# Loading and multiplying the first tiles of x and W by halves of columns

## The chip, the cores and the metric

The kernel runs on one core of a Trainium2 chip. The metric is the device time of one execution in microseconds (us), and the kernel's time is the median of several executions.

## The reference

Four layers with residuals, in float32, on x of shape (32, 64, 1024). What is computed, cut to what matters:

```python
x = x + einsum('bct,bcd->bdt', x, L0_w[itok_B_0_15])          # 16 matrices of 64x64
x = x + einsum('bct,bcd->bdt', x, L1_w[itok_B_0_15])          # 16 matrices of 64x64
x = x + einsum('bsi,oi->bso', x, W) + low_rank(x, A[itok_B_0_2], B) * 0.5   # W is 1024x1024
x = x + einsum('bsi,boi->bso', x, L3_w[itok_B_3_7])           # 8 matrices of 1024x1024
```

The indices pick a matrix for each of the 32 batches. A residual becomes an identity matrix added to the weights.

## The kernel before, in words

A float32 product is made of three matmuls in the faster fp32r type: each operand is split into a high part (a copy rounded to fp32r) and a low part (the operand less its high part), and hi·hi, hi·lo and lo·hi are summed in PSUM. High parts are made mostly by ScalarE (ACT; `w_hi`, `x_hi`), low parts by VectorE (DVE; `w_lo`, `x_lo`).

The third layer's product with W comes first in the program. It works on transposed tiles: W in blocks of four tiles of 128x512 (`w_slot`), x in blocks of four tiles of 128x512 (`x_slot`), and one block product is 4 outputs (`o`) x 4 tiles (`k`) x 3 parts = 48 matmuls of 128x512. The blocks are combined as in a fast 2x2 matrix product, with the sums S1 to S4 and T1 to T4. Low-rank terms (`low_rank`, L1400) and deltas (L1412) go between. The fourth layer follows from some 182 us on (L1517), with each batch's own matrix, and the first two layers, joined to one 64x64 matrix per index (L1449 makes these), are applied to its result (`mix`, L1543).

Every engine runs its own program, and what orders them are semaphores, written by hand. A wait stands in an engine's program and holds everything behind it there. At the start:

- **SP (the sync engine)** issues the loads in the order of its code, L307 to L322: for each of the four tiles k of the first W block and the first x block a load of 256 KB, the loads of the two small layers' weights (`w1_s`, `w0_s`, 256 KB each) behind k = 1, then `load_x(1, 1, 1)` (1 MB, the second x block), `lora_a`, `load_x(2, 2, 0)`, `lora_b`, `load_w(1, 1, 2)` and two more blocks of W. There is no wait among them.
- **ACT** issues five loads of its own, L564 to L568: the first tile of x, the identity `eye`, the indices `toks`, and `asked` and `cells`, which the plan of the fourth layer is made from. Then comes its first activation, L662, ahead of which the compiler has put a table load, and which makes the high part of columns 128 to 511 of W's tile k = 0 (`w_hi_off`). Columns 0 to 127 follow (L664, `w_hi`) when DVE has added the identity to them. For k = 1 to 3 it makes `w_hi` and `x_hi` (L573, L576).
- **DVE** casts the first tile of x (L878, `x_hi`), waits for the identity, and goes through k = 0 to 3: `x_lo`, the identity added to the next tile of W (`diagonal`, L1179, semaphore `A11`), `w_lo`, and for k = 1 and 2 `plus_eye` (L886, semaphore `w01i`), which adds identities to `w1_s` and `w0_s`. At k = 2 and 3 it also loads four indices each into registers (L1194). `x_los(1)` follows, the second x block's low part (L906), and later the selection of low-rank matrices (L1204).
- **PE (TensorE)** multiplies zeros (`warm`, L1354, WARM = 15 matmuls of 128x256 on the tile `st`), then makes the first product (L1439): for each k the four hi·hi, the four hi·lo, the four lo·hi. For k = 0 it takes the outputs in the order 1, 2, 3, 0, since output 0 needs the columns with the identity. L1449 joins the two small layers (it waits for `w01i`), and the next product (L1373 to L1375) waits for the low parts of the second x block.

`cells` and `asked` are waited for by the semaphore `consts`, just ahead of the first steps of the plan (DVE, L1219), and `eye` by DVE ahead of `diagonal(0)`.

## Time and profile before

| | us |
|---|---|
| median of 3 runs | 383.66 (383.42 to 383.82) |
| the profiled execution's own time | 382.85 |
| its span, first to last instruction | 381.05 (the page rounds to 381.1) |
| PE busy in the span | 375.2 |
| first matmul of zeros | 1.35 |
| first matmul of the first product | 5.03 |
| start of L1449, behind the first product | 16.64 |

The span is 1.8 us shorter than the execution's own time, and that execution was 0.81 us below the median of the runs. Times inside the trace are counted from the start of the span. A busy PE is not PE at its peak: matmuls are pipelined, so the distance from one start to the next tells more than the duration of one.

### The profile page before, as it was taken

To read this page: it belongs to the slowest core of one execution; us is meant where nothing else is said; L and a number is where in the kernel's file an instruction comes from. 1 tells how busy PE (TensorE), PEld (TensorE's weight loads), DVE (VectorE), ACT (ScalarE), POOL (GpSimd) and SP (SyncE) were. 2 spreads that over 40 slices of the span, in tenths; PEclk is the share of its full clock that TensorE was granted. 3 is DMA by queue.
4 is the path that set the end of the run, shared out by engine and by line. 5 is a ranking of instruction groups with operands and counts; after the bars stand their busy time and mean duration, and the time that the engine had idled before them with its cause. 6 is when DMAs were issued, how large, how long until landed. Compare 5 with 4: busy or idle time off the path is not lost.

```text
span 381.1 us, 7667 instructions
## 1 busy us (share of the span) xinstructions
PE 375.2 (98%) x1733; PEld 312.9 (82%) x1734; DVE 268.4 (70%) x301; ACT 224.7 (59%) x299; POOL 116.4 (31%) x157
## 2 busy tenths in 40 slices
PE   8999999999999999999999999999999999999995
PEld 7888888888888888888888888888888888888884
DVE  4786978846849788537868467963599635999653
ACT  4689577487246475245475465753677536779433
POOL 0000231000000000024765347763167532676500
PEclk9999999999999999999999999999999999999999
DMA  8976905640278384406428316552256522664223
GB/s 286 397 281 212 341 0 193 208 151 9 104 251 279 133 330 139 169 26 215 161 71 252 86 28 206 192 164 58 57 190 210 160 58 58 207 201 151 60 65 85
DMA packets 24187, 61.38 MB, mean 161 GB/s; under 512 B 1906, under 2 KB 2098, under 8 KB 24114
## 3 DMA queue, kind: packets, MB, share of 16 engines
q1 hardware_dynamic: 23648, 60.10, 47.7%
q8 instruction: 29, 0.48, 0.5%
q10 hardware_dynamic: 466, 0.44, 0.4%
q14 instruction: 44, 0.36, 0.3%
HBM read 52.15 MB, written 8.39 MB: 159 GB/s over the span
## 4 chain that ended last, share of the span: by engine, by line
PE 98%; ACT 1%; ACTq 1%; issue 0%
PE ps L1517 45%; PE ps L1373 12%; PE ps L1374 12%; PE ps L1375 12%; PE ps L1400 4%; PE ps L1543 4%; PE ps L1439 3%; PE ps L1609 2%; PE ps L1412 2%; PE ps L1558 1%; ACT L662 0%; PE ps L1449 0%; ACTq L566 0%; ACT ring L662 0%; ACTq L568 0%
## 5 line engine op out<-in xcount | busy, mean ns | idle before, releaser
L1517 PE MATMUL ps<-ring,aT 128*128 x752 | 173.1, 389 | 0.0
L1517 PEld LDWEIGHTS ps<-ring,aT 128*128 128x128 f32 x752 | 141.1, 188 | 29.5 <-issue 0.2
L1373 PE MATMUL ps<-ring 128*128 128x512 f32 x208 | 81.1, 390 | 0.0
L1374 PE MATMUL ps<-ring 128*128 128x512 f32 x208 | 81.0, 389 | 0.0
L1375 PE MATMUL ps<-ring 128*128 128x512 f32 x208 | 80.9, 389 | 0.0
L476 POOL TENSOR_TENSOR aT<-xT,aT 128x512 fp32r<-128x512 f32 (+1 forms) x36 | 55.5, 1562 | 46.8 <-ACT aT L761 41.6
L1266 DVE TENSOR_TENSOR ring<-raw,ring 128x1024 f32 (+1 forms) x40 | 63.2, 1639 | 5.9 <-ACT ring L747 5.9
L767 ACT ACTIVATE aT<-ps 64x1024 fp32r<-64x1024 f32 x32 | 32.7, 1023 | 48.5 <-PE ps L1517 48.2
L1294 DVE TENSOR_TENSOR stage<-ps,stage 64x1024 f32<-64x1024 f32 x30 | 36.7, 1222 | 27.7 <-ACT stage L776 27.0
L1283 DVE TENSOR_TENSOR aT<-ps,aT 64x1024 fp32r<-64x1024 f32 x32 | 39.1, 1223 | 21.4 <-ACT aT L767 20.7
L1373 PEld LDWEIGHTS ps<-ring 128*128 128x128 f32 x208 | 39.1, 188 | 8.1
L1375 PEld LDWEIGHTS ps<-ring 128*128 128x128 f32 x208 | 39.0, 188 | 8.1
L1374 PEld LDWEIGHTS ps<-ring 128*128 128x128 f32 x208 | 39.1, 188 | 7.9
L776 ACT ACTIVATE stage<-ps 64x1024 f32<-64x1024 f32 x30 | 30.5, 1018 | 23.8 <-PE ps L1543 23.4
L747 ACT ACTIVATE ring<-raw 128x1024 f32 (+1 forms) x40 | 39.2, 1046 | 6.0 <-POOL raw L468 3.5
L630 ACT ACTIVATE xT<-ps 128x512 f32<-128x512 f32 x40 | 22.4, 593 | 20.0 <-PE ps L1375 19.7
L525 POOL MEMSET st<- 128x512 f32 x1 | 0.5, 525 | 100.3 <-ACT low_split L623 100.3
L468 POOL TENSOR_TENSOR raw<-raw,eye 128x128 f32<-128x128 f32 x40 | 18.9, 485 | 25.3 <-DMA raw<-w3t 22.4
L906 DVE TENSOR_TENSOR ring<-ring_f,ring 128x1024 fp32r<-128x1024 f32 (+1 forms) x20 | 21.5, 1113 | 5.1 <-ACT ring L576 5.1
L761 ACT ACTIVATE aT<-xT 128x512 fp32r (+1 forms) x36 | 20.0, 601 | 3.2 <-DVE xT L987 2.8
L576 ACT ACTIVATE ring<-ring_f 128x1024 fp32r<-128x1024 f32 (+1 forms) x19 | 17.9, 984 | 6.2 <-DMA ring_f<-xt 3.6
L490 POOL CAST st<-aT 128x64 fp32r x32 | 18.7, 583 | 8.8 <-POOL st L492 6.5
(95 smaller groups left out, 329.2 us busy)
## 6 DMA issues: line engine op xcount, KB each, us to landing
raw<-w3t SPq DMA_DIRECT2D x40, 512.0 KB, 4.3
ring_f<-xt SPq DMA_DIRECT2D x8, 1024.0 KB, 7.9
raw<-xt SPq DMA_DIRECT2D x8, 1024.0 KB, 5.2
out<-stage SPq DMA_DIRECT2D x30, 256.0 KB, 3.2
ring_f<-wt SPq DMA_DIRECT2D x4, 1024.0 KB, 8.0
xT<-xt SPq DMA_DIRECT2D x3, 1024.0 KB, 10.2
xT<-wt SPq DMA_DIRECT2D x2, 1024.0 KB, 16.0
ring_f<-wt SPq DMA_DIRECT2D x4, 256.0 KB, 4.7
```

What stands on the lines that cost most here:

```text
L476: pool.tensor_tensor(x3_split(i, ks, P + h * T, T), xT[:, ks, bass.ds(which[h] * T, T)], as_f32(x3_split(i, ks, h * T, T)), ALU.subtract). ...
L630: act.activation(dst[:, o, :], ps_l2(phase, j, o), ACT.Copy).then_inc(s(name), 1)
L747: act.activation(dst, adapter_raw(t), ACT.Copy).then_inc(s("w_hi"), 1)
L767: act.activation(r_tile(h)[own, :], acc(p)[own, :, :].rearrange("p a n -> p (a n)"), ACT.Copy)\
L776: act.activation(stage[own, p, :], mixed_ps[h][other, :, :].rearrange("p a n -> p (a n)"), ACT.Copy)\
L1266: dve.tensor_tensor(in_two(unit_of(t, 1)), adapter_raw(t), as_f32(in_two(unit_of(t, 0))), ALU.subtract)\
L1283: dve.tensor_tensor(r_tile(h)[other, :], acc(p)[own, :, :].rearrange("p a n -> p (a n)"), as_f32(r_tile(h)[own, :]), ALU.subtract).then_in ...
L1294: dve.tensor_tensor(dst, mixed_ps[h][own, :, :].rearrange("p a n -> p (a n)"), dst, ALU.add)\
L1373: pe.matmul(dst, hi_of(qw)[:, k, cs], hi_of(qx)[:, k, :], start=start and k == 0, stop=False, skip_group_check=True)
L1374: pe.matmul(dst, hi_of(qw)[:, k, cs], lo_of(qx)[:, k, :], start=False, stop=False, skip_group_check=True)
L1375: last = pe.matmul(dst, lo_of(qw)[:, k, cs], hi_of(qx)[:, k, :], start=False, stop=stop and k == HALF - 1, skip_group_check=True)
L1517: last = pe.matmul(acc(i)[:, n, :], x3_split(i, k, start, P), ring[:, bass.ds(off + (part * D + n * 512), 512)], start=(k == 0 and j == 0) ...
```

## The change

It touches only the beginning of each engine's program.

1. The first tile (k = 0) of W and that of x are loaded in two halves of 256 columns each (`FRONT`), W's second half first. The semaphores are `w_front1`, `w_front0`, `x_front0`, `x_front1`. Both queues so issue one more load ahead of what followed.
2. On SP, tiles k = 1 to 3 follow at once, and `w1_s`, `w0_s` come behind them. `asked` and `cells` move from ACT's queue to SP's, behind `w0_s` and ahead of `load_x(1, 1, 1)`.
3. ACT makes the high part of W's columns 256 to 511 as soon as they are there, and then of 128 to 255. Each raises `w_hi_off` by one.
4. DVE casts x by halves, makes `x_lo` of tile 0 before it waits for the identity, and does both `plus_eye` behind the last tile's `w_lo`.
5. PE has 12 matmuls of zeros in place of 15, and in the first product for k = 0 outputs 2 and 3 (W's second half) come first, each in two matmuls of 256 columns for hi·hi. Output 1 follows, then hi·lo of 2, 3 and 1, both for output 0, and lo·hi in the order 2, 3, 1, 0. From k = 1 on the order is as before.

```diff
-WARM = 15
+WARM = 12
+FRONT = slice(0, 256), slice(256, 512)
...
-            for k in range(HALF):
+            for half in (1, 0):
+                sp.dma_start(raw_of(w_slot(0))[:, 0, FRONT[half]], wt[1, 1, 0][:, FRONT[half]]).then_inc(s(f"w_front{half}"), 16)
+            for k in range(1, HALF):
                 one = slice(k, k + 1)
                 sp.dma_start(raw_of(w_slot(0))[:, one, :], w_block(1, 1)[:, one, :]).then_inc(s(f"w_in0_{k}"), 16)
-
-                if k:
-                    sp.dma_start(raw_of(x_slot(0))[:, one, :], x_block(1, 0)[:, one, :]).then_inc(s(f"x_in0_{k}"), 16)
-                if k == 1:
-                    sp.dma_start(w1_s, w1).then_inc(s("w1"), 16)
-                    sp.dma_start(w0_s, w0t).then_inc(s("w0"), 16)
+                sp.dma_start(raw_of(x_slot(0))[:, one, :], x_block(1, 0)[:, one, :]).then_inc(s(f"x_in0_{k}"), 16)
+            sp.dma_start(w1_s, w1).then_inc(s("w1"), 16)
+            sp.dma_start(w0_s, w0t).then_inc(s("w0"), 16)
+            sp.dma_start(asked[:, :], indices[:, 2, :].to_broadcast([B, B])).then_inc(s("consts"), 16)
+            sp.dma_start(cells[:, 0:C_SIZE], plan_c).then_inc(s("consts"), 16)
...
-            act.dma_start(raw_of(x_slot(0))[:, 0, :], xt[0, 1, 0]).then_inc(s("x_in0_0"), 16)
+            for half in range(2):
+                act.dma_start(raw_of(x_slot(0))[:, 0, FRONT[half]], xt[0, 1, 0][:, FRONT[half]]).then_inc(s(f"x_front{half}"), 16)
             act.dma_start(eye[:, :], eye_c).then_inc(s("eye"), 16)
             act.dma_start(toks[:, :, :], indices).then_inc(s("toks"), 16)
-            act.dma_start(asked[:, :], indices[:, 2, :].to_broadcast([B, B])).then_inc(s("consts"), 16)
-            act.dma_start(cells[:, 0:C_SIZE], plan_c).then_inc(s("consts"), 16)
...
-            act.wait_ge(s("w_in0_0"), 16)
-            act.activation(hi_of(w_slot(0))[:, 0, P:], raw_of(w_slot(0))[:, 0, P:], ACT.Copy).then_inc(s("w_hi_off"), 1)
+            for half, cols in ((1, FRONT[1]), (0, slice(P, 2 * P))):
+                act.wait_ge(s(f"w_front{half}"), 16)
+                act.activation(hi_of(w_slot(0))[:, 0, cols], raw_of(w_slot(0))[:, 0, cols], ACT.Copy).then_inc(s("w_hi_off"), 1)
...
-            dve.wait_ge(s("x_in0_0"), 16)
-            dve.tensor_copy(hi_of(x_slot(0))[:, 0, :], raw_of(x_slot(0))[:, 0, :]).then_inc(s("x_hi"), 1)
-            dve.wait_ge(s("eye"), 16)
+            for half, raised in enumerate(("x_hi_front", "x_hi")):
+                dve.wait_ge(s(f"x_front{half}"), 16)
+                dve.tensor_copy(hi_of(x_slot(0))[:, 0, FRONT[half]], raw_of(x_slot(0))[:, 0, FRONT[half]]).then_inc(s(raised), 1)
...
+            x_lo(0, None, slice(0, 1))
+            dve.wait_ge(s("eye"), 16)
             diagonal(0)
...
-                if k in (1, 2):
-                    plus_eye(k - 1)
+                if k == HALF - 1:
+                    plus_eye(0)
+                    plus_eye(1)
...
+            pe.wait_ge(s("w_hi_off"), 1)
+            pe.wait_ge(s("x_hi_front"), 1)
+            for o in (2, 3):
+                part(o, 0, 0, 0, FRONT[0], True)
+            pe.wait_ge(s("x_hi"), 1)
+            for o in (2, 3):
+                part(o, 0, 0, 0, FRONT[1])
+            pe.wait_ge(s("w_hi_off"), 2)
+            part(1, 0, 0, 0, start=True)
+            pe.wait_ge(s("x_lo"), 1)
+            for o in (2, 3, 1):
+                part(o, 0, 0, 1)
+            pe.wait_ge(s("w_hi"), 1)
+            part(0, 0, 0, 0, start=True)
+            part(0, 0, 0, 1)
+            pe.wait_ge(s("w_lo"), 1)
+            for o in (2, 3, 1, 0):
+                part(o, 0, 1, 0)
```

ACT's program from its first load to its first three activations, before (ring_f is the memory that W and x are loaded to, ring that of the split parts):

```order
L564 DMA ring_f<-xt 128x512
L565 DMA eye<-eye_c 128x192
L566 DMA toks<-indices 1x96
L567 DMA asked<-indices 32x32
L568 DMA cells<-plan_c 32x81
L662 ACT_TABLE_LOAD
L662 ACTIVATE ring<-ring_f 128x384 [waits w_in0_0]
L664 ACTIVATE ring<-ring_f 128x128 [waits A11]
L573 ACTIVATE ring<-ring_f 128x512 [waits A11]
```

The same stretch of ACT's program in the changed kernel:

```order
L567 DMA ring_f<-xt 128x256 x2
L568 DMA eye<-eye_c 128x192
L569 DMA toks<-indices 1x96
L664 ACT_TABLE_LOAD
L664 ACTIVATE ring<-ring_f 128x256 [waits w_front1]
L664 ACTIVATE ring<-ring_f 128x128 [waits w_front0]
L666 ACTIVATE ring<-ring_f 128x128 [waits A11]
L574 ACTIVATE ring<-ring_f 128x512 [waits A11]
```

Two loads stand no longer ahead of the table load, one more half of x does, and the first activation has become two.

PE's program from the matmuls of zeros to the second tile (k = 1) of the first product, before:

```order
L1354 MATMUL ps<-st 128x256 [waits zeroed]
L1354 MATMUL ps<-st 128x256 x14
L1439 MATMUL ps<-ring 128x512 [waits x_hi,w_hi_off]
L1439 MATMUL ps<-ring 128x512 x2
L1439 MATMUL ps<-ring 128x512 [waits w_hi]
L1439 MATMUL ps<-ring 128x512 [waits x_lo]
L1439 MATMUL ps<-ring 128x512 x3
L1439 MATMUL ps<-ring 128x512 [waits w_lo]
L1439 MATMUL ps<-ring 128x512 x3
L1439 MATMUL ps<-ring 128x512 [waits x_hi,w_hi]
```

The same stretch of PE's program in the changed kernel:

```order
L1360 MATMUL ps<-st 128x256 [waits zeroed]
L1360 MATMUL ps<-st 128x256 x11
L1430 MATMUL ps<-ring 128x256 [waits x_hi_front,w_hi_off]
L1430 MATMUL ps<-ring 128x256
L1430 MATMUL ps<-ring 128x256 [waits x_hi]
L1430 MATMUL ps<-ring 128x256
L1430 MATMUL ps<-ring 128x512 [waits w_hi_off]
L1430 MATMUL ps<-ring 128x512 [waits x_lo]
L1430 MATMUL ps<-ring 128x512 x2
L1430 MATMUL ps<-ring 128x512 [waits w_hi]
L1430 MATMUL ps<-ring 128x512
L1430 MATMUL ps<-ring 128x512 [waits w_lo]
```

Columns multiplied are as many as before. The wait for `w_hi`, which needs the identity, stood behind three matmuls of 512 columns and stands now behind what makes six of them.

DVE's program at tile k = 0, in the changed kernel (before, L1179, the identity's addition with its wait for `eye`, stood ahead of the first L906, which is L908 here):

```order
L881 CAST ring<-ring_f 128x256 [waits x_front0]
L881 CAST ring<-ring_f 128x256 [waits x_front1]
L908 TENSOR_TENSOR ring<-ring_f,ring 128x512 [waits x_hi]
L1181 TENSOR_TENSOR ring_f<-ring_f,eye 128x128 [waits w_front0,eye]
L1181 TENSOR_TENSOR ring_f<-ring_f,eye 128x128 [waits w_in0_1]
L901 TENSOR_TENSOR ring<-ring_f,ring 128x512 [waits w_hi]
```

## Rows read from the trace of the kernel before

**Rows 1.** The page: span, busy time of PE, and 40 slices of the span
```profile
span 381.1 us, 7667 instructions
...
PE 375.2 (98%) x1733; PEld 312.9 (82%) x1734; DVE 268.4 (70%) x301; ACT 224.7 (59%) x299; POOL 116.4 (31%) x157
...
PE   8999999999999999999999999999999999999995
```

**Rows 2.** The chain that ended last: start us, us, what
```profile
3.11 1.28 ACT L662
4.39 0.01 issue
4.40 0.53 ACT ring L662
4.94 0.09 issue
5.03 11.68 PE ps L1439 x48
16.71 1.09 PE ps L1449 x16
...
182.16 16.32 PE ps L1517 x72
```

**Rows 3.** Timeline of ACT's queue: start us, us, engine, line, what
```profile
0.79 0.41 ACTq L564 DMA_DIRECT2D ring_f<-xt  x1
1.24 0.44 ACTq L565 DMA_DIRECT2D eye<-eye_c  x1
...
2.28 0.32 ACTq L567 DMA_DIRECT2D asked<-indices  x1
...
2.64 0.44 ACTq L568 DMA_DIRECT2D cells<-plan_c  x1
...
5.80 0.31 ACT L664 ACTIVATE ring<-ring_f 128x128 fp32r<-128x128 f32 x1 [0.88 <-DVE ring_f L1179]
```

**Rows 4.** Timeline of DVE at the first product
```profile
4.45 0.43 DVE L878 CAST ring<-ring_f 128x512 fp32r<-128x512 f32 x1 [4.34 <-DMA ring_f<-xt]
...
5.48 0.29 DVE L1179 TENSOR_TENSOR ring_f<-ring_f,eye 128x128 f32<-128x128 f32 x1 [0.60 <-DMA eye<-eye_c]
5.69 0.69 DVE L906 TENSOR_TENSOR ring<-ring_f,ring 128x512 fp32r<-128x512 f32 x1
...
15.36 2.36 DVE L906 TENSOR_TENSOR ring<-ring_f,ring 128x1024 fp32r<-128x1024 f32 x2 [1.30 <-ACT ring L576]
```

**Rows 5.** Timeline of PE in small windows: zeros, then the first product's start
```profile
1.35 3.57 PE L1354 MATMUL ps<-st 128*128 128x256 f32 x15 [1.35 <-POOL st L457]
...
1.94 1.05 PE L1354 MATMUL ps<-st 128*128 128x256 f32 x4
...
5.59 0.84 PE L1439 MATMUL ps<-ring 128*128 128x512 f32 x2
...
6.02 0.65 PE L1439 MATMUL ps<-ring 128*128 128x512 f32 x2
```

**Rows 6.** DMA issues in small windows: KB each, us from issue to landing
```profile
ring_f<-wt SPq DMA_DIRECT2D x1, 256.0 KB, 3.5
ring_f<-xt ACTq DMA_DIRECT2D x1, 256.0 KB, 3.6
...
eye<-eye_c ACTq DMA_DIRECT2D x1, 96.0 KB, 4.2
...
ring_f<-wt SPq DMA_DIRECT2D x1, 256.0 KB, 4.1
```

**Rows 7.** Stretches: us, busy us of PE, PEld, DVE, ACT, POOL; PEclk, DMA share, GB/s
```profile
1.80:2.20 0.40, 0.40 (x4) 0.40 (x4) 0.00 (x0) 0.00 (x0) 0.00 (x0) 1.00 0.97 108
2.20:2.60 0.40, 0.40 (x4) 0.40 (x4) 0.00 (x0) 0.00 (x0) 0.00 (x0) 1.00 0.85 215
2.60:3.00 0.40, 0.40 (x3) 0.40 (x3) 0.00 (x0) 0.00 (x0) 0.00 (x0) 1.00 0.75 266
3.00:3.40 0.40, 0.40 (x3) 0.40 (x3) 0.00 (x0) 0.29 (x1) 0.00 (x0) 1.00 0.99 374
3.40:3.80 0.40, 0.40 (x4) 0.40 (x3) 0.00 (x0) 0.40 (x1) 0.00 (x0) 1.00 1.02 384
...
6.00:10.00 4.00, 4.00 (x19) 3.14 (x18) 3.37 (x8) 2.42 (x5) 0.00 (x0) 1.00 1.03 391
```

More of the change, by code:

```diff
@@ L1176, in diagonal @@
             def diagonal(k):
-                dve.wait_ge(s(f"w_in0_{k}"), 16)
+                dve.wait_ge(s(f"w_in0_{k}" if k else "w_front0"), 16)
                 d = raw_of(w_slot(0))[:, k, P * k:P * (k + 1)]
                 dve.tensor_tensor(d, d, eye[:, 0:P], ALU.add).then_inc(s("A11"), 1)
+            x_lo(0, None, slice(0, 1))
+            dve.wait_ge(s("eye"), 16)
             diagonal(0)
@@ L1184, in _ @@
                 one = slice(k, k + 1)
-                x_lo(0, None, one)
+                if k:
+                    x_lo(0, None, one)
                 if k < HALF - 1:
@@ L1422, in _, with part @@
             w, x = (hi_of(w_slot(0)), lo_of(w_slot(0))), (hi_of(x_slot(0)), lo_of(x_slot(0)))
-            for k in range(HALF):
-                for a, b in ((0, 0), (0, 1), (1, 0)):
-                    high = (a, b) == (0, 0)
-                    if high and k == 0:
-                        pe.wait_ge(s("w_hi_off"), 1)
-                        pe.wait_ge(s("x_hi"), 1)
-                    elif high:
-                        pe.wait_ge(s("w_hi"), k + 1)
-                        pe.wait_ge(s("x_hi"), k + 1)
-                    elif b:
-                        pe.wait_ge(s("x_lo"), k + 1)
-                    else:
-                        pe.wait_ge(s("w_lo"), k + 1)
-                    for o in (1, 2, 3, 0) if high and k == 0 else range(HALF):
-                        if high and k == 0 and o == 0:
-                            pe.wait_ge(s("w_hi"), 1)
-                        last = pe.matmul(ps_l2(0, 0, o), w[a][:, k, P * o:P * (o + 1)], x[b][:, k, :],
-                                         start=high and k == 0, stop=k == HALF - 1 and a == 1, skip_group_check=True)
-                        if k == HALF - 1 and a:
-                            last.then_inc(s("l2"), 1)
+            def part(o, k, a, b, cols=slice(0, CT), start=False):
+                return pe.matmul(ps_l2(0, 0, o)[:, cols], w[a][:, k, P * o:P * (o + 1)], x[b][:, k, cols],
+                                 start=start, stop=k == HALF - 1 and a == 1, skip_group_check=True)
@@ new lines, in _ @@
+            part(0, 0, 0, 0, start=True)
[3 more added lines that the diff above has]
+                part(o, 0, 1, 0)
+            for k in range(1, HALF):
+                pe.wait_ge(s("w_hi"), k + 1)
+                pe.wait_ge(s("x_hi"), k + 1)
+                for o in range(HALF):
+                    part(o, k, 0, 0)
+                pe.wait_ge(s("x_lo"), k + 1)
+                for o in range(HALF):
+                    part(o, k, 0, 1)
+                pe.wait_ge(s("w_lo"), k + 1)
+                for o in range(HALF):
+                    last = part(o, k, 1, 0)
+                    if k == HALF - 1:
+                        last.then_inc(s("l2"), 1)
```

## The prediction

> **What bounds the kernel now.** I read the page first. PE is busy for 375.2 of 381.1 us, and in every slice but the first and the last it stands at 9 tenths [rows 1]. So an edit at the start is worth what it takes off the time at which PE gets through its first work, as long as no later wait takes it back. The chain of waits says what holds PE until 5.03 us [rows 2]: ACT's table load from 3.11 us, the copy that makes the high part of W's first tile from 4.40, 0.09 us to the matmul, and then 48 matmuls in 11.68 us. Ahead of the table load stand ACT's five DMA issues, from 0.79 on [rows 3]. DVE's branch is as long: its cast starts at 4.45, when x has landed, and ends at 4.88 [rows 4]. Both must get shorter for a gain.
>
> Next, PE's pace. In the fourth layer 72 matmuls of 512 columns take 16.32 us [rows 2], 0.227 us each. That is the 2.4 GHz level. The matmuls of zeros have 256 columns and start (1.05 - 0.415) / 3 = 0.21 us apart [rows 5], which is the 1.2 GHz level (0.415 us is what a single one lasts: 1.05 is three steps and one duration), although the column PEclk shows 1.00 [rows 7]. The first product starts at 5.03, the next matmuls at 5.59 and 6.02, the fourth at 6.27 [rows 2, 5]. The steps are 0.56, 0.43 and 0.25: two matmuls at the lower level, the first with 0.13 us on top, and the higher level from about 6.02 to 6.05 us, some 4.7 us after PE's first matmul. **So PE is slow where the change makes it start earlier**, and time won there is worth about half. From 6.27 on, 45 matmuls at 0.227 would end at 16.48; L1449 follows at 16.64. Later waits in this product cost 0.1 us at most.
>
> **The change, part by part.**
>
> *ACT's queue.* Two DMA issues leave, 0.32 and 0.44 us with 0.03 between (0.82). One more half of x comes, as long as the first (0.41 + 0.04), since an issue's time hardly follows its size: 96 KB take 0.44, 10 KB also 0.44 [rows 3]. The table load so starts 0.37 us earlier, at 2.74, and ends at 4.02. Bounds for the new issue: 0.32 and 0.44, that is 4.0 or 4.05.
>
> *The first copy of W.* 384 columns take 0.52 us [rows 2] and 128 take 0.31 [rows 3], so 256 take 0.42. It ends at 4.44 if W's half is there by 4.02. The matmul came 0.11 us behind the old copy's start plus 0.52, so the first one is now at **4.55 in place of 5.03**.
>
> *Do the halves land in time?* The whole tiles land at 0.77 + 3.5 = 4.3 (W) and 0.79 + 3.6 = 4.4 (x) [rows 6]. From 1.8 us on DMA moves 108, 215, 266, 374 and 384 GB/s in steps of 0.4 us [rows 7]. The sum reaches 256 KB, two halves, at some 3.05 us, and 512 KB, both tiles, at 3.75; landing is 0.5 to 0.7 us behind that. If bytes decide, the first halves land near 3.7 and the second ones at 4.3 and 4.4. If the number of loads decides, halves land where the first and second loads of each queue do now: 4.3 and 4.4, then 1.22 + 4.1 = 5.3 (the second on SP's queue) and 1.24 + 4.2 = 5.4 (`eye`, the second on ACT's) [rows 3, 6]. I take the bytes, as the rates climb to what the queues move later, 391 GB/s [rows 7].
>
> The Trainium skill speaks against splitting here ("DMA: Bandwidth & Descriptors", section Bandwidth): it wants loads of 1 MiB or more, with 64 KB at 138 GB/s against 341 for 1 MB, measured for loads that GpSimd issues. At 138 GB/s the four halves would take 3.8 us, and by that estimate the kernel would lose about 1 us. This trace doesn't agree for loads that queue up: with pieces of 256 KB in the queues it moves 391 GB/s [rows 7]. 128 KB it doesn't show.
>
> *DVE's casts.* 512 columns take 0.43 us [rows 4]. A half takes between 0.21 and 0.43. I take 0.28. The first ends at about 4.0 and does not bind, the second at 4.4 + 0.3 = 4.7.
>
> *PE in the first product.* At the lower level: first half matmul at 4.55, the next at 4.90 (0.21 + 0.13), then 5.11 (its `x_hi` is there at 4.8), 5.32, output 1 at 5.54, hi·lo at 5.96. The clock has risen meanwhile, so the next one starts at about 6.21. By then the equivalent of 4 matmuls of 512 columns is done. Before it was 3 at 6.27. **Gain: 0.06 + 0.227 = 0.28 us.** The half matmuls add no columns. Three matmuls of zeros fewer only make room: 12 of them let PE go at 1.35 + 0.38 + 11 x 0.21 = 4.1, ahead of 4.55; 15 would have held it until 4.72.
>
> *Waits behind it.* `x_lo` takes 0.69 [rows 4]: 4.75 to 5.44, asked for at 5.96. `eye` lands at 5.4 to 5.5 as now, since as many bytes are ahead of it, or at 6.0 if it counts as third load. Then diagonal 0.29 and ACT's copy 0.31 give `w_hi` at 6.2 (6.6), asked for at 6.67. `w_lo` (0.69) is there at 7.0 (7.3), asked for at 7.12, so between nothing and 0.2 us is lost. DVE has `x_lo` now ahead of the identity, so PE is not held by that. Tiles 2 and 3 land two loads earlier, which wins nothing, since PE did not wait for them.
>
> *What lands later.* SP issues one half, `asked` and `cells` more before the second x block, some 1.2 us of issue time; that block is issued at about 6.4 in place of 5.2 and still stands in a queue that is full until 10 us (391 GB/s) [rows 7], so it lands as before or 0.1 later. Both `plus_eye` now stand ahead of `x_los(1)`, 1.4 us of DVE. Before, DVE idled for 1.30 us ahead of that step [rows 4] while its sequencer loaded indices, so this is covered. If it were not, `x_los(1)`, which now starts at 15.36 and has its first half at 16.6, would have it at 18.0 in the worst case; PE asks at 17.4, so 0.6 us would be lost. `cells` is wanted only beyond 31 us.
>
> Sum: 381.05 - 0.28 = 380.77 us of span, 382.57 of own time. The profiled execution was 0.81 below the median, so the forecast for the median is 383.66 - 0.28 = **383.38 us**.
>
> **Rivals.**
>
> *B, more than half comes through.* If PE stands at the higher level when the product starts, the two slow matmuls vanish as well: 0.48 + 0.56 (1.24 us for three starts against 0.68) = 1.04 us, 382.6. It needs a rise before 4.6 us. Against it: in this trace PE had worked since 1.35 and was still slow at 5.6 [rows 5]. For it: one execution is all I see, and the runs differ by 0.4 us among themselves and by up to 1 from this one.
>
> *C, the second halves land late* (the number of loads decides; here stands the skill's rule). The first matmul is then at 4.8 (x's half at 4.4, cast 0.28, 0.1). x's second half lands at 5.4 and is cast at 5.7, hi·hi of outputs 2 and 3 ends at 6.2, output 1 at 6.4, `x_lo` is there at 6.5, three matmuls to 7.2, two to 7.65, `w_lo` at 7.75 because `eye` came at 6.0, four to 8.65. Before, twelve matmuls had been passed at 6.27 + 9 x 0.23 = 8.35. That is 0.3 us slower: 383.95. It decides if halves land more than 0.6 us behind the wholes.
>
> *D, slower: the clock rises later.* There are three matmuls of zeros fewer and a new pause, 4.1 to 4.55 us, against 0.3 us before. Each us at the lower level costs 1 - 0.227/0.427 = 0.47 us. If the pause made PE start its wait anew, the rise would come 4.7 us behind 4.55, at 9.2 in place of 6.0: + 1.5 - 0.28 = 1.2 us, 384.9. It outweighs the gain from 0.6 us of delay on, and is a loss over 0.2% from 2.2 us. Against it: a pause of 0.3 us (4.72 to 5.03) did no harm, and the work begins at the same 1.35. The Trainium skill ("TensorE: Matmul & The Clock Gate", part 1) says that the monitor runs freely and does not start anew with the kernel. By that rule the moment of the rise wanders from run to run in both kernels and D is unlikely; one trace cannot show it.
>
> *E, nothing is won*, because the table load doesn't end earlier or the stretch at 17 us gives it back: 383.66, inside the forecast's own range.
>
> **How the numbers follow.** A difference of 0.2% (0.77 us) is about what a measurement can tell from none. The forecast with E has 0.62, and its gains run from 0 to 0.6 us; 0.03 of it I give to gains above 0.77. B has 0.17, C 0.12, D 0.09. So faster 0.20, same 0.59 + 0.12 = 0.71, slower 0.09. The range reaches down to B (382.6) and up past C with the 0.2 us by which the runs differ from their median (384.2).
>
> **What would show it.** In the changed profile: the table load starts near 2.74 and the first product at 4.55, the steps of the first matmuls are 0.35, 0.21, 0.21, 0.21, 0.43, then 0.23, with the change of level near 6.0, and L1449 starts at 16.35. Wrong would be: halves of x that land after 4.8 (C), steps of 0.43 beyond 6.5 us (D), a first step of 0.12 (B), idle PE ahead of L1449 or of the second product (the moved `plus_eye`), or a gain at 16.6 that is gone by 182 us.

## The result, and the profile of the changed kernel

| | before | changed |
|---|---|---|
| median, us | 383.56 (382.80 to 383.82, 14 runs) | 383.87 (383.29 to 385.07, 14 runs) |
| profiled execution's own time / span, us | 382.85 / 381.05 | 383.86 / 382.0 |
| first matmul of the first product | 5.03 | 4.54 |
| start of the two small layers' join (L1449, now L1471) | 16.64 | 17.28 |
| start of the last matmul | 376.46 | 377.40 |

The ratio of the changed kernel to the one before is 1.0017, 95% interval 1.0010 to 1.0024. So the changed kernel is **slower**: by 0.3 us if the two medians are compared, by 0.65 us if the ratio is taken, which is not the quotient of the two medians (that is 1.0008). Either is less than the 0.2% which the prediction calls no difference, and the time is inside its range, but the sign is not the one forecast, and the interval of the ratio excludes 1. The two profiled executions are 1.0 us apart, because that of before was a quick one (0.7 us below its median); the changed kernel's stands at its median.

The page of the changed kernel, for [rows 1]:

```profile
span 382.0 us, 7669 instructions
...
PE 375.2 (98%) x1732; PEld 311.8 (82%) x1733; DVE 267.3 (70%) x302; ACT 225.2 (59%) x300; POOL 116.6 (31%) x157
...
PE   7999999999999999999999999999999999999995
```

PE has the same work in a longer span, and the one slice that differs is the first, 7 tenths in place of 8. The chain of waits, for [rows 2], names what fills it:

```profile
1.71 4.83 DMA eye<-eye_c
6.57 0.30 DVE ring_f L1181
6.90 0.32 ACT ring L666
7.26 10.09 PE ps L1430 x42
17.35 1.09 PE ps L1471 x16
...
182.81 16.32 PE ps L1539 x72
```

The table load and the first copy of W are gone from the chain. In their place stands one transfer, the identity's, issued at 1.71 us and landed at 6.55, then the addition, the copy and PE at 7.26. The 72 matmuls at the head of the fourth layer start 0.65 us later than before and take the same 16.32: nothing of the start is taken back, and nothing is added between. From the join to the last matmul the two executions need 360.12 and 359.82 us, and those of the experiments 359.8 to 360.2, with one exception told below, so 0.3 us there is scatter.

The timeline of the changed kernel (start us, us, engine, line, what, and in brackets the idle time before and its releaser), for [rows 3 to 5]:

```profile
1.71 0.45 ACTq L568 DMA_DIRECT2D eye<-eye_c  x1
...
2.78 1.28 ACT L664 ACT_TABLE_LOAD   x1 [2.65 <-issue]
...
3.50 0.29 DVE L881 CAST ring<-ring_f 128x256 fp32r<-128x256 f32 x1 [3.39 <-DMA ring_f<-xt]
...
4.07 0.61 ACT L664 ACTIVATE ring<-ring_f 128x256 fp32r<-128x256 f32 x2
4.43 0.30 DVE L881 CAST ring<-ring_f 128x256 fp32r<-128x256 f32 x1 [0.64 <-DMA ring_f<-xt]
...
4.54 1.93 PE L1430 MATMUL ps<-ring 128*128 128x256 f32 x8 [0.26 <-ACT ring L664]
...
4.76 0.69 DVE L908 TENSOR_TENSOR ring<-ring_f,ring 128x512 fp32r<-128x512 f32 x1
...
6.57 0.49 DVE L1181 TENSOR_TENSOR ring_f<-ring_f,eye 128x128 f32<-128x128 f32 x2 [1.12 <-DMA eye<-eye_c]
...
7.26 10.09 PE L1430 MATMUL ps<-ring 128*128 128x512 f32 x42 [0.79 <-ACT ring L666]
...
14.39 1.29 DVE L888 TENSOR_TENSOR stage<-stage,eye 128x512 f32<-128x512 f32 x2
...
15.85 2.36 DVE L908 TENSOR_TENSOR ring<-ring_f,ring 128x1024 fp32r<-128x1024 f32 x2 [0.17 <-issue]
```

The start did what the change says: table load at 2.78, casts of 0.29 and 0.30 us, first product at 4.54. Then DVE sits idle for 1.12 us and PE for 0.79 until the identity has come. Both `plus_eye` (1.29 us) lie ahead of `x_los(1)`, which starts at 15.85 with 0.17 us of idle time before it: covered.

PE in small windows (a row lists the matmuls that touch its window; its first number is the start of the first of them):

```profile
4.54 0.63 PE L1430 MATMUL ps<-ring 128*128 128x256 f32 x3 [0.26 <-ACT ring L664]
...
4.76 0.75 PE L1430 MATMUL ps<-ring 128*128 128x256 f32 x4
...
5.12 0.88 PE L1430 MATMUL ps<-ring 128*128 128x512 f32 x2
...
5.84 0.63 PE L1430 MATMUL ps<-ring 128*128 128x512 f32 x2
...
7.60 0.88 PE L1430 MATMUL ps<-ring 128*128 128x512 f32 x2
...
7.98 0.73 PE L1430 MATMUL ps<-ring 128*128 128x512 f32 x2
...
8.32 0.86 PE L1430 MATMUL ps<-ring 128*128 128x512 f32 x3
```

The second row starts at 4.76 and the third, three starts on, at 5.12: 0.12 us for a matmul of 256 columns, where the zeros of [rows 5] took 0.21. The trace records the rise of the granted clock at 4.57, so in this execution PE stood at the 2.4 GHz level from its first product matmul on. The last of the eight matmuls that can go without the identity starts at 6.08; 0.23 us behind it, at 6.31, PE wants `w_hi` and gets it at 7.26. That is **0.95 us of waiting**.

From there the whole loss can be added up. The eight matmuls are as many columns as six of 512, and before PE was through six at 6.27 + 3 x 0.23 = 7.0. So at 6.31 PE is 0.69 us ahead: 0.49 of it come from the earlier start, the rest from the clock. Then it waits 0.95. The next three steps, from 7.26 to 8.32, take 1.06 us where three at 0.23 take 0.69, so 0.37 more are lost. In the middle of them PE waits for `w_lo`, which DVE starts only at 7.24, when `w_hi` is there, and which takes 0.69:

```profile
7.24 0.69 DVE L901 TENSOR_TENSOR ring<-ring_f,ring 128x512 fp32r<-128x512 f32 x1 [0.17 <-ACT ring L666]
```

The sum is -0.69 + 0.95 + 0.37 = +0.63 us, and the join is 0.64 late.

The issues of the changed kernel (KB each, us from issue to landing), for [rows 6]:

```profile
ring_f<-xt ACTq DMA_DIRECT2D x2, 128.0 KB, 2.9
...
ring_f<-wt SPq DMA_DIRECT2D x1, 128.0 KB, 2.9
eye<-eye_c ACTq DMA_DIRECT2D x1, 96.0 KB, 4.8
```

By the trace's packets the halves of W landed at 3.31 and 4.12, those of x at 3.48 and 4.41. The identity's parts lie on 16 DMA engines: the first was through at 5.00, the last at 6.55, and the semaphore wants all. The third load on SP's queue, W's tile k = 1, came as late: issued at 1.70, it landed at 6.37, where before, as second load, it had landed at 5.28. The stretches for [rows 7] (PEclk, DMA share and GB/s at the end):

```profile
3.80:4.40 0.60, 0.48 (x3) 0.18 (x1) 0.00 (x0) 0.59 (x3) 0.00 (x0) 1.00 0.91 288
4.40:5.00 0.60, 0.46 (x3) 0.46 (x4) 0.53 (x2) 0.29 (x2) 0.00 (x0) 1.00 1.05 302
```

Before, the first two of these stretches moved 378 and 384 GB/s. The transfers dip for a while here, and some single packets (three of them between 4.3 and 4.8 us) take 0.8 to 0.9 us.

### The profile page after: what moved, and what is told of

The parts are those of the page before. It is cut to its first block, busy times and chain, and to the rows that moved or that the text cites. A ratio compares the mean times of both kernels' runs of the same rounds, so it can differ in the third digit from the quotient of the medians.

```text
span 382.0 us, 7669 instructions
## 1 busy us (share of the span) xinstructions
PE 375.2 (98%) x1732; PEld 311.8 (82%) x1733; DVE 267.3 (70%) x302; ACT 225.2 (59%) x300; POOL 116.6 (31%) x157
## 4 chain that ended last, share of the span: by engine, by line
PE 97%; DMA 1%; ACTq 0%; ACT 0%; issue 0%; DVE 0%
PE ps L1539 45%; PE ps L1379 12%; PE ps L1380 12%; PE ps L1381 12%; PE ps L1406 4%; PE ps L1565 4%; PE ps L1430 3%; PE ps L1631 2%; PE ps L1418 2%; DMA eye<-eye_c 1%; PE ps L1580 1%; PE ps L1471 0%; ACTq L567 0%; ACT stage L852 0%; ACT ring L666 0%
## 5 line engine op out<-in xcount | busy, mean ns | idle before, releaser
L478 POOL TENSOR_TENSOR aT<-xT,aT 128x512 fp32r<-128x512 f32 (+1 forms) x36 | 56.7, 1594 | 45.5 <-ACT aT L763 42.2
L1272 DVE TENSOR_TENSOR ring<-raw,ring 128x1024 f32 (+1 forms) x40 | 62.1, 1609 | 6.2 <-ACT ring L749 6.2
L470 POOL TENSOR_TENSOR raw<-raw,eye 128x128 f32<-128x128 f32 x40 | 19.7, 505 | 26.2 <-DMA raw<-w3t 22.4
L908 DVE TENSOR_TENSOR ring<-ring_f,ring 128x1024 fp32r<-128x1024 f32 (+1 forms) x20 | 21.5, 1114 | 5.0 <-ACT ring L577 4.8
L492 POOL CAST st<-aT 128x64 fp32r x32 | 17.6, 551 | 9.1 <-POOL st L494 6.8
```

What stands on the lines that cost most here:

```text
L478: pool.tensor_tensor(x3_split(i, ks, P + h * T, T), xT[:, ks, bass.ds(which[h] * T, T)], as_f32(x3_split(i, ks, h * T, T)), ALU.subtract). ...
L1272: dve.tensor_tensor(in_two(unit_of(t, 1)), adapter_raw(t), as_f32(in_two(unit_of(t, 0))), ALU.subtract)\
```

## The experiments

The theories, as the expectations number them: **I**, the identity is late, because splitting x's tile made it the third load of ACT's queue; **II**, the fewer zeros and the clock; **III**, the moved loads (`w1_s`, `w0_s`, `asked`, `cells`) and `plus_eye`; **IV**, the halves themselves; **V**, whatever stands third on the queue is late, the identity or another load. The table gives for each kernel where the identity stands, when it lands (issue plus the row's time to landing), when the join of the small layers starts, and the ratio to the kernel before in the same job.

| kernel | identity | lands | join | median us (runs) | ratio, 95% |
|---|---|---|---|---|---|
| before | 2nd on ACT | 5.4 | 16.64 | 383.56 (14) | 1 |
| changed | 3rd on ACT | 6.5 | 17.28 | 383.87 (14) | 1.0017 (1.0010 to 1.0024) |
| e1, 15 zeros | 3rd on ACT | 6.1 | 16.89 | 383.54 (11) | 1.0014 (1.0004 to 1.0024) |
| e2 | 3rd on SP | 4.8 | 16.35 | 383.39 (11) | 1.0005 (0.9996 to 1.0014) |
| e3, moves only | 2nd on ACT | 5.2 | 16.36 | 383.27 (11) | 1.0004 (0.9995 to 1.0013) |
| e4, halves only | 3rd on ACT | 6.4 | 17.17 | 383.97 (12) | 1.0025 (1.0011 to 1.0039) |
| f1, before | last on ACT | 8.6 | 22.47 | 387.66 (4) | 1.0109 (1.0094 to 1.0124) |
| f2 | 2nd on ACT, ahead of x's second half | 4.4 | 21.07 | 386.66 (6) | 1.0082 (1.0064 to 1.0100) |
| f3 | GpSimd's queue | 5.1 | 16.45 | 382.90 (11) | 0.9990 (0.9981 to 0.9999) |
| f4 | 3rd on SP, x's k = 1 on ACT | 6.4 | 17.43 | 383.76 (12) | 1.0015 (0.9999 to 1.0032) |
| g1, x whole | 2nd on ACT | 4.9 | 16.44 | 383.25 (11) | 1.0002 (0.9993 to 1.0011) |
| g2, wholes | GpSimd's queue | 5.4 | 16.61 | 383.25 (12) | 1.0003 (0.9995 to 1.0012) |
| g3, f3 with 15 zeros | GpSimd's queue | 5.1 | 16.35 | 383.25 (11) | 0.9993 (0.9984 to 1.0002) |
| g4, changed again | 3rd on ACT | 7.3 | 18.08 | 384.56 (12) | 1.0033 (1.0015 to 1.0051) |

The kernel before had medians of 383.28, 383.24 and 383.34 us (35, 23 and 35 runs) in the three jobs e, f and g, against 383.56 in the job of the result. So kernels of different jobs are compared by their ratios. Landings and joins are of one profiled execution each: e2, e3 and g1 have joins 0.2 to 0.3 us ahead of the kernel before and yet ratios of 1.0002 to 1.0005, so a difference of that size between two joins says nothing about the medians.

### e1: the changed kernel with 15 matmuls of zeros

```diff
-WARM = 12
+WARM = 15
```

> The changed kernel with 15 matmuls of zeros in place of 12. Theory I (the identity): PE's early start is worth nothing, because output 0 needs the identity, which now stands third on ACT's queue, and its slowest DMA engine landed at 6.55 us against 5.46 before; 0.18 us of later start are hidden in that wait. Expected as the changed kernel, 383.9 (383.6 to 384.1). Theory II (the clock): the three missing matmuls let the clock rise later; then this is faster than the changed kernel, near 383.5.

Median 383.54, ratio 1.0014, still slower than before. The rows of its timeline:

```profile
4.71 1.84 PE L1430 MATMUL ps<-ring 128*128 128x256 f32 x8
...
6.18 0.49 DVE L1181 TENSOR_TENSOR ring_f<-ring_f,eye 128x128 f32<-128x128 f32 x2 [0.64 <-DMA eye<-eye_c]
...
6.87 2.84 PE L1430 MATMUL ps<-ring 128*128 128x512 f32 x10 [0.31 <-ACT ring L666]
```

The three more zeros hold the product's start until 4.71, and PE has no pause ahead of it. DVE waits for the identity all the same. The pause between zeros and product is not the cause of the wait, and II falls as the explanation of the loss. The median of 383.54 is near the number that II had named, but the kernel before was 0.28 us quicker in this job too, and the ratios of e1 and of the changed kernel (1.0014 and 1.0017) are not told apart. Whether three matmuls of zeros are worth something smaller, these runs do not show.

### e2: the identity third on SP's queue instead

```diff
+            sp.dma_start(eye[:, :], eye_c).then_inc(s("eye"), 16)
             for k in range(1, HALF):
...
-            act.dma_start(eye[:, :], eye_c).then_inc(s("eye"), 16)
```

> The changed kernel with the identity's load moved from ACT's queue to SP's, behind the two halves of W and ahead of tile k = 1. ACT's table load then ends near 3.6 and the first matmul starts near 4.1. Theory I: the identity lands by 5.3, PE doesn't idle at output 0, 383.0 (382.7 to 383.3). Theory II: PE starts even earlier behind the same few matmuls of zeros, 383.9 or slower. Theory III (tiles and constants moved on SP's queue hurt something later): no help, 383.9.

The identity landed at 4.8, 3.1 us behind its issue, and the join started at 16.35, which is what the forecast for the changed kernel says. The join is 0.93 us ahead of the changed kernel's, and the kernel is no longer told apart from before (1.0005). The table load came a further 0.5 us earlier (2.29), and the first product at 4.07.

```profile
2.29 1.28 ACT L664 ACT_TABLE_LOAD   x1 [2.16 <-issue]
...
4.07 5.55 PE L1430 MATMUL ps<-ring 128*128 128x256 f32 x20
4.60 0.29 DVE L881 CAST ring<-ring_f 128x256 fp32r<-128x256 f32 x1 [0.81 <-DMA ring_f<-xt]
```

x's second half now sets PE's pace: it is cast at 4.60, and PE's third half matmul starts at 4.95. So a still earlier start of the product is worth little. For theory I the kernel went the way it should, but no further than back to the time of before: 383.39 us is just above the range that had been expected (382.7 to 383.3).

### e3 and e4: the two parts of the change alone

e3 is the kernel before with the moved loads and `plus_eye`; e4 is the changed kernel with those undone.

```diff
             for k in range(HALF):
...
-                if k == 1:
-                    sp.dma_start(w1_s, w1).then_inc(s("w1"), 16)
-                    sp.dma_start(w0_s, w0t).then_inc(s("w0"), 16)
+            sp.dma_start(w1_s, w1).then_inc(s("w1"), 16)
+            sp.dma_start(w0_s, w0t).then_inc(s("w0"), 16)
+            sp.dma_start(asked[:, :], indices[:, 2, :].to_broadcast([B, B])).then_inc(s("consts"), 16)
+            sp.dma_start(cells[:, 0:C_SIZE], plan_c).then_inc(s("consts"), 16)
...
-                if k in (1, 2):
-                    plus_eye(k - 1)
+                if k == HALF - 1:
+                    plus_eye(0)
+                    plus_eye(1)
```

> The kernel before with the moved loads alone: w1, w0, asked and cells behind the first product's tiles on SP's queue, both plus_eye behind the last tile; whole tiles, 15 matmuls of zeros. The identity stays second on ACT's queue. Theory I: it lands at 5.5 as before, the start moves by under 0.1 us because x's tile lands at 4.4, so 383.5 (383.3 to 383.7). Theory III: as slow as the changed kernel, 383.9.

> The changed kernel with the loads of w1, w0, asked and cells back where they were (halves, PE's order and 12 matmuls of zeros alone). The table load ends near 4.8 and the first matmul starts near 5.4. Theory I: the identity is third on ACT's queue and lands at 6.0 to 6.6, so as slow as the changed kernel, 383.9 (383.7 to 384.2). Theory III: 383.5, as before.

e3: ratio 1.0004, not told from before. The moved parts cost nothing, and III falls. e4: 1.0025, slower. Its timeline has what is most telling here:

```profile
3.59 1.28 ACT L665 ACT_TABLE_LOAD   x1 [3.46 <-issue]
...
5.36 4.40 PE L1430 MATMUL ps<-ring 128*128 128x256 f32 x17 [1.08 <-ACT ring L665]
6.46 0.49 DVE L1182 TENSOR_TENSOR ring_f<-ring_f,eye 128x128 f32<-128x128 f32 x2 [1.12 <-DMA eye<-eye_c]
```

With six issues ahead of it the table load starts at 3.59 and the product at 5.36, which is 0.82 us later than in the changed kernel; and yet the join starts at 17.17, 0.11 us earlier than there. **When the product starts makes no difference, because the identity sets when it goes on.**

### f1: the kernel before with the identity last on ACT's queue

```diff
-            act.dma_start(eye[:, :], eye_c).then_inc(s("eye"), 16)
             act.dma_start(toks[:, :, :], indices).then_inc(s("toks"), 16)
...
             act.dma_start(cells[:, 0:C_SIZE], plan_c).then_inc(s("consts"), 16)
+            act.dma_start(eye[:, :], eye_c).then_inc(s("eye"), 16)
```

> The kernel before with the identity's load moved behind toks, asked and cells on ACT's queue, nothing else. Theory I (a late identity is what costs): it lands at 6.1 to 6.8 in place of 5.5, PE idles ahead of output 0, and the kernel is 0.3 to 0.8 us slower than before. Theory IV (the halves themselves, their extra descriptors and matmuls, cost the time): no difference to before.

387.66 us, ratio 1.0109: the direction is right, the size is far above what was expected. The identity was issued at 2.63 and took 6.0 us to land. Its chain, and stretches of it:

```profile
2.63 6.04 DMA eye<-eye_c
...
9.38 8.63 PE ps L1439 x25
```

```profile
8.30:15.00 6.70, 5.62 (x13) 4.51 (x14) 5.68 (x12) 3.57 (x7) 0.00 (x0) 0.50 1.04 399
15.20:17.00 1.80, 1.80 (x10) 1.46 (x9) 1.11 (x3) 1.80 (x3) 0.00 (x0) 1.00 1.05 390
```

PE's fourth matmul starts at 9.38 in place of 6.27, 3.1 us late. The column PEclk then reads 0.50: the granted clock fell to the 1.2 GHz level at 8.27 and came back at 15.10. The 5.7 us from 9.38 to there, at 0.47 us lost for each, are 2.7 more, and 3.1 + 2.7 = 5.8 is what the join is late (22.47 against 16.64). A pause of over 3 us was paid nearly twice. This execution was the slowest of only four, 1.3 us above their median; by the medians f1 loses 4.4 us.

### f2: the identity between the halves of x

```diff
             for half in range(2):
                 act.dma_start(raw_of(x_slot(0))[:, 0, FRONT[half]], xt[0, 1, 0][:, FRONT[half]]).then_inc(s(f"x_front{half}"), 16)
-            act.dma_start(eye[:, :], eye_c).then_inc(s("eye"), 16)
+                if not half:
+                    act.dma_start(eye[:, :], eye_c).then_inc(s("eye"), 16)
```

> The changed kernel with the identity between the two halves of x on ACT's queue. The identity lands by 4.5, x's second half takes the third place. Theory I in its narrow form (only the identity's wait matters): 0.3 to 0.5 us faster than the changed kernel. Theory V (any load in third place is caught by a stretch of slow DMA packets between 4 and 6 us, so that what matters is what stands there): x's second half lands at 5.0 to 6.4, PE waits for it at its third matmul, and nothing is won, 383.9 or slower.

Second on the queue, the identity lands at 4.4. Now the second half of x is third, and it lands at 7.46, 5.75 us behind its issue, and PE's third half matmul follows at 7.83:

```profile
1.71 5.75 DMA ring_f<-xt
```

```profile
7.80:12.90 5.10, 5.07 (x13) 4.18 (x14) 3.94 (x9) 2.50 (x5) 0.00 (x0) 1.00 1.06 399
12.90:15.00 2.10, 2.10 (x10) 1.72 (x10) 0.83 (x3) 1.36 (x3) 0.00 (x0) 1.00 1.02 402
```

It is not the identity that is slow, but what stands third on ACT's queue; that is theory V of the expectation. Nor is it ACT's queue alone: the third load on SP's, W's tile k = 1, landed at 7.28 here. Here too the pause is paid twice: 13 matmuls in 5.1 us up to 12.90, and 10 in 2.1 behind it. The higher level came only then: from 8.43 to 12.70 the matmuls start 0.43 us apart, and the trace records the rise at 12.90. The column PEclk reads 1.00 in both rows, as it does in all these traces ahead of the first change on record, so there the steps have to be read and not the column.

### f3: the identity on GpSimd's queue

```diff
             pool.memset(st[:, :, :, :].bitcast(F32), 0.0).then_inc(s("zeroed"), 1)
+            pool.dma_start(eye[:, :], eye_c).then_inc(s("eye"), 16)
...
-            act.dma_start(eye[:, :], eye_c).then_inc(s("eye"), 16)
```

> The changed kernel with the identity's load issued by GpSimd behind its first memset, on a queue of its own. Table load from 2.3 to 3.6, first matmul at 4.1. Theory I: if it lands before 5.3, as the version with the identity on SP's queue or up to 0.2 us faster than that; if GpSimd's queue is slow and it lands past 6, as slow as the changed kernel.

382.90 us, ratio 0.9990 (0.9981 to 0.9999): the only kernel of this study whose interval lies below 1, by 0.34 us of median. It does so by 0.0001, and with twelve kernels compared that is weak evidence. But it has all the halves and is not slower, so the halves themselves are not what made the changed kernel lose, and IV falls. Its timeline:

```profile
1.35 0.68 POOL L460 DMA_DIRECT2D eye<-eye_c  x1
...
5.28 0.29 DVE L1181 TENSOR_TENSOR ring_f<-ring_f,eye 128x128 f32<-128x128 f32 x1
...
6.17 0.29 DVE L1181 TENSOR_TENSOR ring_f<-ring_f,eye 128x128 f32<-128x128 f32 x1 [0.60 <-DMA ring_f<-wt]
...
7.12 1.06 PEld L1430 LDWEIGHTS ps<-ring 128*128 128x128 f32 x5 [0.49 <-DVE ring L901]
```

DVE adds the identity at 5.28, right behind `x_lo`, without waiting. The next wait shows: the addition for tile k = 1, which DVE has ahead of `w_lo` of k = 0, waits 0.60 us for W's tile k = 1, and PE waits 0.49 for `w_lo`. The tile is the third load on SP's queue and landed at 6.14, so the late third load is still there and only another consumer meets it. That may be why a product which starts at 4.09, 0.94 us earlier than before, gives only a third of a us; no run removed this wait as well.

### f4: the identity third on SP, x's tile k = 1 on ACT's queue

```diff
+            sp.dma_start(eye[:, :], eye_c).then_inc(s("eye"), 16)
...
-            act.dma_start(eye[:, :], eye_c).then_inc(s("eye"), 16)
+            act.dma_start(raw_of(x_slot(0))[:, 1, :], xt[0, 1, 1]).then_inc(s("x_in0_1"), 16)
```

> The version with the identity on SP's queue behind the halves of W, with the x tile of k = 1 issued by ACT behind the halves of x. In the profile of that version the x tile of k = 1 was fifth on SP's queue and landed at 7.2, and its high part held PE at 8.0. Expected: it lands near 6, no idle PE at k = 1; the first matmul at 4.5. 0.1 to 0.3 us faster than the kernel before. If the start of PE counts for more than these waits, slower than the version with the identity on SP's queue.

Missed. The identity stands where it stood in e2 and is issued at the same 1.70, but takes 4.7 us to land instead of 3.1:

```profile
eye<-eye_c SPq DMA_DIRECT2D x1, 96.0 KB, 4.7
```

What differs is that 256 KB of x stand third on ACT's queue and have left SP's. So the place on its own queue alone doesn't decide; what the other queue has in flight at the time counts too, or the engine's luck in that one execution: 15 of the 16 DMA engines were through with the identity by 5.30, the last at 6.42. The join at 17.43 is 0.26 us behind that of e4 with the same landing, because here DVE waits 0.44 us for W's tile k = 1 as well, ahead of `w_lo`.

### g1: x's first tile whole, W's in halves

```diff
-            for half in range(2):
-                act.dma_start(raw_of(x_slot(0))[:, 0, FRONT[half]], xt[0, 1, 0][:, FRONT[half]]).then_inc(s(f"x_front{half}"), 16)
+            act.dma_start(raw_of(x_slot(0))[:, 0, :], xt[0, 1, 0]).then_inc(s("x_front"), 16)
...
-                dve.wait_ge(s(f"x_front{half}"), 16)
+                dve.wait_ge(s("x_front"), 16)
```

> The changed kernel with x's first tile in one load again (W's in halves), so that the identity is second on ACT's queue, as before the change. Theory I/V (what is third on a queue lands 1 us later than what is second): the identity lands at 5.2 to 5.5, the first matmul at 4.8, and the kernel is 0.3 to 0.6 us faster than the changed kernel, 383.2 (382.9 to 383.4). If the identity's place is not what makes the changed kernel slow: 383.7.

The same bytes on the same queues as in the changed kernel, in one load less ahead of the identity. It lands at 4.9 and the join starts at 16.44; 1.0002, no longer slower.

```profile
eye<-eye_c ACTq DMA_DIRECT2D x1, 96.0 KB, 3.7
```

This is the most direct measurement of the failed step: bytes ahead of it being equal, the identity needs 3.7 us from its issue as second load and 4.8 as third. It is also issued 0.47 us earlier. The runs agree with it inside one job, 1.0002 here against 1.0033 for g4, and the intervals are apart. A rival is that halves move in packets of 1 KB where wholes have 2 KB, so that the changed kernel has 128 packets more ahead of the identity than g1. It is too small: the median packet of 1 KB took 46 ns and that of 2 KB 84 ns, which over 16 engines makes 0.06 us of the 1.1.

### g2 and g3: what the halves and the zeros are worth with the identity out of the way

g2 is e3 with the identity on GpSimd's queue (whole tiles, 15 zeros); g3 is f3 with 15 zeros.

```diff
-WARM = 12
+WARM = 15
```

> Whole first tiles and the moved loads as in the version without halves, and the identity on GpSimd's queue. Without halves the first matmul is at 4.7 to 4.9. If the halves are of use once the identity is out of their way, this is 0.1 to 0.3 us slower than the version with halves and the identity on GpSimd's queue (382.9), so 383.1 to 383.2; if PE's early start at the lower clock level is worth nothing, both are the same.

> The version with halves and the identity on GpSimd's queue, with 15 matmuls of zeros. PE is free at 4.71 in place of 4.09. If time won at the start before the clock rises is worth about half of itself: 0.1 to 0.3 us slower, 383.1. If other waits in tile k = 0 absorb it: the same, 382.9.

g2 has 1.0003 and a first matmul at 5.08 although its table load begins at 1.82: x is cast at 4.50, so whole tiles bind there and a short queue brings nothing by itself. f3 has 0.9990. Halves together with an early identity look worth about 0.1%, but the two come from different jobs and their intervals just overlap, and in the job of the g kernels g1, g2 and g3 have the same median, 383.25. So this is not shown. g3 (0.9993) is not told from f3, which has 12 zeros, nor, by its interval, from before. Its profiled execution has a gap of 1.2 us at 359 us that none of the others has, and that no edit here touches; without it its last matmul would start within 0.2 us of e2's.

### g4: the changed kernel once more

> The changed kernel itself again, for a second look at where its identity lands and for a comparison on the same chip. Theory I: the identity lands at 6.1 to 6.6 again and PE idles for 0.5 to 1.2 us ahead of output 0; 383.5 to 383.9.

The same code as the changed kernel, in the job of the g kernels. The ratio is 1.0033 (1.0015 to 1.0051), so the loss holds; the runs go from 382.92 to 387.52 us where those of the kernel before lie within 382.76 and 383.81. The median is above the expected 383.5 to 383.9. What varies shows in the profile:

```profile
4.54 2.93 PE L1430 MATMUL ps<-ring 128*128 128x256 f32 x8 [0.26 <-ACT ring L664]
...
7.33 0.49 DVE L1181 TENSOR_TENSOR ring_f<-ring_f,eye 128x128 f32<-128x128 f32 x2 [1.95 <-DMA eye<-eye_c]
...
8.02 1.70 PE L1430 MATMUL ps<-ring 128*128 128x512 f32 x5 [0.55 <-ACT ring L666]
```

The start is the same to 0.01 us; the identity landed at 7.3 this time, later than the expected 6.1 to 6.6. PE was at the lower level here (clock up at 7.51), so its eight matmuls took until 7.27 and it waited 0.75 us.

## Why the prediction was wrong, point by point

- **The start: right.** Table load 2.78 (forecast 2.74), first product 4.54 (4.55), DVE's half cast 0.29 (0.28), first half of x cast at 3.50 and the second from 4.43 (4.4), so bytes decide for the halves and not the number of loads. `x_lo` ended at 5.45 (5.44). By the rate for 64 KB in the Trainium skill ("DMA: Bandwidth & Descriptors", section Bandwidth) the prediction estimates 3.8 us for the four halves. In this trace it is 2.6 us, from their first packet at 1.80 to the last landing at 4.41, as late as the whole tiles landed before (4.43): for pieces of 128 KB in a queue it does not agree.
- **The failed step: "`eye` lands at 5.4 to 5.5 as now, since as many bytes are ahead of it, or at 6.0 if it counts as third load".** Four executions with it third on ACT's queue give 6.1, 6.4, 6.5 and 7.3; with one load less and the same bytes (g1) it is 4.9. The other bound, 6.0, was right in kind, but it is little more than the 0.47 us of the later issue on top of 5.46. The landing is that of the slowest of 16 DMA engines, and this one is 1.5 us behind the first (5.00 and 6.55). The forecast's `w_hi` at 6.2 (6.6) became 7.2. The time lost behind it, 0 to 0.2 us in the forecast, became 0.95 for `w_hi` and 0.37 in the three steps after it.
- **The wait became larger than the gain.** At 6.31 PE was 0.69 us ahead, and 1.32 were lost by 8.32; e4 shows that with the identity late a start at 4.54 or at 5.36 comes to the same.
- **The join at 16.35** was forecast for an identity that lands at 5.4 to 5.5. Where it lands at 4.8 to 5.2 (e2, e3, g1, f3, g3) the join starts at 16.35 to 16.45; in the changed kernel at 17.28, 0.93 later than the forecast.
- **The clock: a single execution taken for the rule.** The forecast had PE at the lower level until 6.05, and a gain of 0.28 instead of 0.48 for it. In the changed kernel the level rose at 4.57, as rival B supposes, and yet nothing was won. That rise was luck: g4 runs the same code and had it at 7.51. B's price of 1.04 us counts no wait for `w_hi`, and there was one. Over the 14 profiled executions the rise lies at 4.6 to 7.5 us, but for f1's fall back and f2's 12.9. With 15 zeros it is at 4.84 to 6.05 (six executions), with 12 at 4.57 to 7.51 (seven): the spans overlap, the earliest of all is the changed kernel's own, and the 9.2 of **rival D** was seen in none of them. D did not make this loss, though g4's 7.51 leaves a smaller delay open. The Trainium skill ("TensorE: Matmul & The Clock Gate", part 1) has the monitor run freely and not start anew with the kernel, and by that rule the same kernel meets the rise at different moments; the 4.57 and 7.51 of the same code agree. It is not the kernel's business alone, and not free of it either: f1 and f2, where PE idled for 3.4 and 2.5 us, are the two that stand apart.
- **Rival C** had the right sign and the right idea, that the count of loads ahead matters, but for the second halves; they landed in time. It named "`eye` came at 6.0" only as one term among its waits. The identity alone, with the halves in time, was the case that should have stood there.
- **The moved loads and `plus_eye`: right.** e3 shows nothing, and `x_los(1)` waits 0.17 us for its own sequencer, not for DVE's work.
- **The sum.** Forecast 383.38 from 383.66, that is -0.28; measured +0.31 between the medians (383.56 and 383.87) and +0.65 by the ratio, which is also what the join of the profiled execution shows (0.64). The forecast's own sum with the wait of 0.95 where 0 to 0.2 stood would have given +0.5 to +0.7, but that it meets the ratio is partly luck: the 0.95 were measured at the higher clock level, where PE asks for `w_hi` at 6.31 and not at 6.67, and the 0.37 are missing. Why the medians show only half is not shown; the identity's landing and the clock differ from one execution to the next.
- **The range held the time, and this is no merit of the working.** It was drawn wide for B and C, and what the centre rests on, that the earlier start comes through, did not happen. The sign failed.

**What stays open.** Why transfers dip between 4 and 6 us and why a single engine falls behind there. The kernels show it at different places; the deepest is in e2 (e3 moved 239 GB/s in the same stretch, before 335):

```profile
5.00:5.60 0.60, 0.60 (x3) 0.60 (x3) 0.60 (x2) 0.00 (x0) 0.00 (x0) 1.00 0.59 123
```

In e2 the identity was through before it. That a third load suffers because it is in flight at that time fits the changed kernel, e1, e2, e4, f2, g1 and g4, but it is only argued: no run moved the dip itself, and f4 shows that the place on a queue does not fix the landing. On SP's queue the third load was late too in most of the kernels with halves (6.37 in the changed kernel, 6.14 in f3, 7.28 in f2, 7.09 in g4), but not in e2 (4.83) and g1 (5.38). This points to DMA engines that serve both queues, and what makes one of them late is open. What the runs show is the step that failed and what the late identity costs, not why it is late.

## What to carry to other kernels

Splitting a load so that its consumer can start earlier pushes everything behind it on that queue one place back. With the same bytes ahead the load behind can still land later, since what counts is its slowest DMA engine (here 1.1 us more from issue to landing). Look up who waits for each load behind the split one, and put a small one that is needed soon on the queue of an engine that is idle; here GpSimd's took the ratio from 1.0017 to 0.9990. Ask of every earlier start what the same engine waits for next, and whether that moved too. And a pause of about 3 us on TensorE near its start cost more than its length in f1 and f2, because the work behind it ran at the lower clock level.

## What the runs showed of the hardware that was not expected

- The landing of one load of 96 KB varied from 3.1 to 6.0 us behind its issue between kernels, and from 4.4 to 5.6 us (e1, e4, the changed kernel, g4) with the queue ahead of it the same or nearly so. x's whole first tile, the first load of that queue, was cast between 4.14 and 4.50 us in the five kernels that have it (before, e3, f1, g1, g2).
- The lateness can lie in one DMA engine of 16: in f4 fifteen were through with the identity by 5.30 us and the last at 6.42.
- A load that GpSimd issues landed as soon as one from the queues of SP or ACT: 3.7, 4.1 and 3.8 us behind its issue (f3, g2, g3), against 4.2 in the kernel before. Its issue took 0.68 us where theirs take 0.45.
- The granted clock fell to 0.50 at 8.27 us in f1, while PE waited from 5.9 to 9.38, and was back only at 15.10, 5.7 us after the work had begun again. In the changed kernel the wait of 0.95 us had no such effect.
